# Moving weight loads and low parts in the prologue of a fused attention and FFN kernel, with unread products in two waits

## The reference

```python
# 1 conditional mixing of the 32 tokens, one matrix and bias a sequence
h = gelu(gelu(cond @ W0 + b0) @ W1 + b1)
att = softmax(h @ W2 + b2)                        # 128 x 8
agg_w = einsum('bk,koi->boi', att, weight)        # 128 x 32 x 32
y = einsum('boi,bih->boh', agg_w, x) + (att @ bias_k)[:, :, None]
# 2 causal attention with rope: 32 query heads, 8 key heads of width 16
x = x + attention(y, Wq, Wk, Wv) @ Wo
# 3 grouped convolution over the features, 9 taps, plus cond @ c_weight.T and a bias
z = conv(x) + ctx
# 4 base product, router, low-rank experts
x = x + z @ base_W.T + base_b + lora(z, A, B, router(z))
```

## Time and profile before

| | before |
|---|---|
| median of 3 runs | 616.13 us (613.89 to 617.95) |
| the profiled execution: time | 615.38 us |
| its span, first to last instruction | 613.6 us |
| PE busy | 585.4 us (95%) |
| DVE busy | 494.0 us (81%) |
| ACT, POOL busy | 221.4 us (36%), 226.7 us (37%) |
| DMA, mean | 116 GB/s |

### The profile page before, as it was taken

The page is one execution under the profiler, slowest core; times in us unless marked ns, Lnnn a source line. Parts: engine busy times, 40 slices in busy tenths (PEclk is TensorE's granted clock), DMA queues, the critical chain, the costliest instruction groups (busy, mean ns, idle before and its releaser), DMA issues.

```text
span 613.6 us, 14243 instructions
## 1 busy us (share of the span) xinstructions
PE 585.4 (95%) x4928; PEld 492.8 (80%) x4928; DVE 494.0 (81%) x1236; ACT 221.4 (36%) x603; POOL 226.7 (37%) x182
## 2 busy tenths in 40 slices
PE   4988999999999999999999999999999999999875
PEld 4666798888888988888889888888898878888664
DVE  4677888888888888888888888888888878888843
ACT  4263334333333333333333333333333333333311
POOL 8164234433333344333333443333334333343310
PEclk9989999999999999999999999999999999999999
DMA  7844454344545543445555434454554344554430
GB/s 195 174 115 114 112 134 127 100 101 106 118 116 133 133 121 98 104 106 118 116 133 133 121 99 104 105 118 116 133 133 121 88 107 104 111 133 111 112 86 36
DMA packets 125206, 71.26 MB, mean 116 GB/s; under 512 B 48781, under 2 KB 107309, under 8 KB 125064
## 3 DMA queue, kind: packets, MB, share of 16 engines
q1 hardware_dynamic: 123696, 70.53, 48.0%
q10 hardware_dynamic: 1352, 0.27, 0.3%
q0 software_dynamic: 144, 0.28, 0.2%
HBM read 51.53 MB, written 19.53 MB: 116 GB/s over the span
## 4 chain that ended last, share of the span: by engine, by line
PE 83%; DVE 6%; DMA 5%; issue 2%; ACT 1%; SPq 1%; ACTq 1%; DVEq 0%
PE ps L420 19%; PE ps L576 15%; PE ps L597 10%; PE ps L603 6%; PE ps L623 5%; DMA scratch<-x_dram 5%; PE ps L524 4%; PE ps L615 4%; PE ps L642 4%; PE ps L662 3%; PE ps L561 3%; PE ps L587 2%; PE ps L631 2%; PE ps L564 2%; PE ps L611 1%
## 5 line engine op out<-in xcount | busy, mean ns | idle before, releaser
L957 POOL TENSOR_TENSOR qk<-network,t 128x640 f32<-128x640 f32 x31 | 48.3, 1560 | 161.2 <-DVE t L1143 161.2
L420 PE MATMUL ps<-wqkv_hi,y_hi 128*128 128x512 f32 (+1 forms) x256 | 88.2, 345 | 3.6 <-DVE raw L1162 2.2
L420 PE MATMUL ps<-wqkv_hi,y_lo 128*128 128x512 f32 (+1 forms) x256 | 88.3, 345 | 0.0
L420 PE MATMUL ps<-wqkv_lo,y_hi 128*128 128x512 f32 (+1 forms) x256 | 88.1, 344 | 0.0
L969 POOL TENSOR_TENSOR raw<-x1p,basebB 128x512 f32<-128x512 f32 x32 | 49.5, 1548 | 58.2 <-DVE x1p L1222 58.2
L755 ACT ACTIVATE raw<-ps 128x512 f32<-128x512 f32 x64 | 37.8, 595 | 74.3 <-PE ps L642 74.2
L964 POOL TENSOR_TENSOR raw<-raw,zero 128x512 f32<-128x512 f32 x32 | 33.3, 1041 | 72.1 <-DVE raw L1211 72.1
L420 PEld LDWEIGHTS ps<-wqkv_hi,y_hi 128*128 128x128 f32 x256 | 49.3, 192 | 11.8 <-DVE raw L1162 3.6
L941 POOL TENSOR_TENSOR raw<-raw,rz 128x512 f32<-128x512 f32 x32 | 33.7, 1052 | 56.4 <-DVE rz L1172 56.4
L420 PEld LDWEIGHTS ps<-wqkv_lo,y_hi 128*128 128x128 f32 x256 | 49.3, 193 | 6.2
L420 PEld LDWEIGHTS ps<-wqkv_hi,y_lo 128*128 128x128 f32 x256 | 49.1, 192 | 6.0
(11 more groups left out here) (185 smaller groups left out, 1459.9 us busy)
## 6 DMA issues: line engine op xcount, KB each, us to landing
scratch<-x_dram SPq DMA_DIRECT2D x96, 256.0 KB, 5.8
x_dram<-x1p SPq DMA_DIRECT2D x32, 260.0 KB, 2.1
xm<-x SPq DMA_DIRECT2D x32, 256.0 KB, 4.4
xr<-x SPq DMA_DIRECT2D x32, 256.0 KB, 2.7
out<-raw SPq DMA_DIRECT2D x32, 256.0 KB, 2.0
v_dram<-vS SPq DMA_DIRECT2D x32, 64.0 KB
vB<-v_dram SPq DMA_DIRECT2D x128, 16.0 KB, 4.9
mixb<-mixb_dram SPq DMA_DIRECT2D x28, 64.0 KB, 3.8
```

The lines of the kernel that those rows point to most:

```text
L420: last = mm(dst, a, b, start=(n == 0), stop=(n == 3 * len(left) - 1))
L957: nc.gpsimd.tensor_tensor(qk[:, :], t1, t2[:, :], ALU.add).then_inc(qk_sb, 1)
```

## The change

It touches the head and the periods -1 to 2 alone; the loop and the tail are the same instructions as before.

- Five products of 128 rows by 512 columns whose result no one reads are put on TensorE ahead of the wait for the softmax of the condition (`att_sb`), four behind `mixing_weights`, three behind `prepare_conv`. Their operand is `z_hi`, which DVE sets to zero first.
- POOL's memsets of `vB`, `x1p`, `cvR` and the pads stand ahead of its wait for the mixing tables (`cwS`), and not behind its copies of them.
- DVE: y of group 0 stands ahead of the low part of Wq's third quarter (`prepare_q(2)`), and `y_lo` ahead of `keep_bias`.
- ACT: the copy of the mixing matrices (`keep_mixing_weights`) stands ahead of `prepare_kv`; the DMAs that pass them on stand behind it.
- SP: the load of Wo stands behind the wait for `mixw_in2`. The load of base_W moves from there to behind the one of group 2's x. The load of lora B, four DMAs in the head, becomes one in period 1, with a DVE copy (`order_lora`) that brings it into the order of the transposes. The load of the mixing matrices of groups 4 to 31 moves from ahead of period 0 into period 1.
- `prepare_ar` moves behind `scores(0)` on TensorE, behind the exponentials on ACT and behind `normalize(0)` on DVE. On ACT the values of group 0 are copied ahead of qT.
- `prepare_base`: phases 0 and 1 move from period 0 to the place in period 1 that phases 2 and 3 had, and 2 and 3 move behind `values(1)`.

```diff
-            for j in range(PH):
-                sp.dma_start(rawB[:, j, :, :], loraB.rearrange("e (p j) r -> j p e r", j=PH)[j]).then_inc(ld["B"], 16)
             sp.wait_ge(y_ps, 1)
@@
-            for k in range(NKV):
-                sp.dma_start(rawo[HD * k:HD * (k + 1), :, :],
-                             Wo.rearrange("(k g d) n -> k d g n", k=NKV, g=NQ)[k]).then_inc(ld["wo"], 16)
@@
             sp.wait_ge(mixw_in2, 16 * NB)
-            sp.dma_start(rawbase, baseW.rearrange("(p j) l -> p j l", j=PH)).then_inc(ld["base"], 16)
+            for k in range(NKV):
+                sp.dma_start(rawo[HD * k:HD * (k + 1), :, :],
+                             Wo.rearrange("(k g d) n -> k d g n", k=NKV, g=NQ)[k]).then_inc(ld["wo"], 16)
@@
             sp.dma_start(xm[:, :], group(x_g, 2)).then_inc(xm_in, 16)
+            sp.dma_start(rawbase, baseW.rearrange("(p j) l -> p j l", j=PH)).then_inc(ld["base"], 16)
@@
-            sp.wait_ge(mixw_out, 16)
-            load_mixw(sp, 4, G, mixw_in)
@@
+                if peeled(t, 1):
+                    sp.dma_start(rawB.rearrange("p e j r -> p e (j r)"), loraB.rearrange("e (p j) r -> p e (j r)", j=PH)
+                                 ).then_inc(ld["B"], 16)
+                    sp.wait_ge(mixw_out, 16)
+                    load_mixw(sp, 4, G, mixw_in)
@@ tensor, head
+            pe.wait_ge(zeros_sb, 1)
+            for _ in range(5):
+                mm(ps[:, 5, :], z_hi[:, 0, :], z_hi[:, :, :].rearrange("p j n -> p (j n)"), start=True, stop=True)
             pe.wait_ge(att_sb, 1)
@@ tensor, steps
-                if peeled(t, 0):
-                    prepare_ar()
@@
                     first_bias()
                     mixing_weights()
+                    unread(4)
@@
                 if live(t):
                     scores(t)
-
+                if peeled(t, 0):
+                    prepare_ar()
                 if peeled(t, 1):
-                    prepare_base((2, 3))
+                    prepare_base((0, 1))
@@
                     prepare_conv()
+                    unread(3)
@@
                 if live(t):
                     values(t)
+                if peeled(t, 1):
+                    prepare_base((2, 3))
@@ gpsimd
             nc.gpsimd.memset(mixw[:, :, :, :], 0.0).then_inc(mixw_zero, 1)
+            nc.gpsimd.memset(zero[:, :], 0.0)
+            nc.gpsimd.memset(vB[:, :, :, :], 0.0)
+            nc.gpsimd.memset(x1p[:, :, :], 0.0)
+            nc.gpsimd.memset(cvR[:, :, :, :, :], 0.0).then_inc(cvZ_sb, 1)
@@ vector, steps
                     prepare_q(0)
-                    prepare_q(2)
                     first_mixing_bias()
@@
                 if peeled(t, -1):
+                    prepare_q(2)
+                    first_y_lo()
                     keep_bias()
-                    first_y_lo()
@@
                     softmax(t)
                     normalize(t)
+                if peeled(t, 0):
+                    prepare_ar()
@@
+            def order_lora():
+
+                dve.wait_ge(ld["B"], 16)
+                v.tensor_copy(phB, rawB.rearrange("p e j r -> p j e r")).then_inc(phB_sb, 1)
```

More of the change, by code:

```diff
@@ L291, in base_bank @@
         def base_bank(j):
-            return (6, 5, 6, 7)[j]
+            return (6, 7, 2, 6)[j]
         def z_transposed():
@@ L455, in first_bias, with unread @@
                 mm(ps[:, 4, 0:S], attT[0:NCOND, :], cbiasS[:, :], start=True, stop=True).then_inc(aggb_ps, 1)
+            def unread(products):
+                for _ in range(products):
+                    mm(ps[:, 5, :], z_hi[:, 0, :], z_hi[:, :, :].rearrange("p j n -> p (j n)"), start=True, stop=True)
             def mixing_weights():
@@ L473, in prepare_base @@
                 for j in phases:
-                    if j >= 2:
-                        pe.wait_ge(base_lo_sb, j - 1)
+                    if j == 3:
+                        pe.wait_ge(base_lo_sb, 1)
                     for jo in range(PH):
@@ L651, in values @@
                     pe.wait_ge(hwT_lo_sb, t - 1)
+                if peeled(t, 0):
+                    pe.wait_ge(prep_sb, 1)
                 if peeled(t, 1):
-                    pe.wait_ge(base_lo_sb, PH)
+                    pe.wait_ge(base_lo_sb, 2)
                 pe.wait_ge(pT_sb, 2 * t + 2)
@@ L841, in steps @@
             def steps(t):
+                if peeled(t, 0):
+                    act.wait_ge(rope_t, 2)
+                    keep_values()
                 if live(t):
@@ L847, in steps @@
                     copy(z_hi[:, :, :].rearrange("p j (q o) -> p j q o", o=CG), z_transposed()).then_inc(z_hi_sb, 1)
-                if peeled(t, 0):
-                    act.wait_ge(rope_t, 2)
-                    keep_values()
-                    prepare_ar()
                 if live(t + 1):
@@ L856, in steps @@
                 if peeled(t, -1):
+                    keep_mixing_weights()
                     prepare_kv()
-                    keep_mixing_weights()
+                    pass_mixing_weights()
                 if peeled(t, 2):
@@ L887, in steps @@
                     copy(heads(oT_hi, 0), heads_ps(0)).then_inc(oT_hi_sb, 1)
-                if peeled(t, 0):
-                    prepare_base((0, 1))
+                if peeled(t, 1):
+                    prepare_base((2, 3))
                 if live(t + 1) and not peeled(t, -1):
@@ L1274, in steps @@
                     conv_bias(t)
+                if peeled(t, 1):
+                    prepare_base((2, 3))
+                    order_lora()
                 if live(t - 2) and not peeled(t, G):
```

32 lines of the change are left out of this document (13 added, 19 removed).

## The result

The changed kernel takes 619.96 us, median of 13 runs (617.80 to 623.80), beside 616.77 (612.59 to 619.05) for the kernel before on the same chip: a ratio of 1.007 with a 95% interval of 1.0046 to 1.0093. It is slower by 0.7%, about 4 us (the medians lie 3.2 us apart). The forecast was 613.6 us with a range to 617.4: the wrong side of no change, and outside the range. One execution of the kernel before, timed beside the experiments, took 1261 us and is left out.

A forecast was written before the change was run, and what follows sets the result against it. It took TensorE's queue of products to bound the kernel, with changes only in the first 60 us. A 0.35 loss less 2.9 gain gave -2.55 on 613.6: span 611.05, time 612.8, median 613.6 us after 0.75; range 611.0 to 617.4.

The forecast's parts named there:

- Head: First stretch: attP 0.75 us sooner, y_lo ended at about 16.4, q and k of group 0 ready at 24.2, not 25.96.
- Mixing blocks: Period 0: their store goes at about 17.35 and they are back 6.3 us later, mixw_in2 at 23.7.
- Wo's landing: Period 0: issues from 23.7 to 27.0, landing 3.5 us after the last, at 30.5; ACT waits 3 us.
- the unlikely case: Wo so late that it costs: blocks take 8.9 us, landing 5.6, Wo there at 35.1, time 618 us; chance 0.09.
- From Wo to the softmax: Period 0: wo_hi, POOL's wo_lo and the normalisation sum to 5.75 us; softmax ready at 36.25, not 37.62.
- The clock: Period 0: TensorE idle from 33.2 to 36.3 us, yet the granted clock full from 36 to 42; no loss booked.
- The rival: Clock falls in the new hole of period 0: costs up to 3.6 us, time 614.8 to 617.2; chance 0.23.
- Said start of the product: Period 0: group 0's product with Wo starts at 39.45 instead of 42.37, a gain of 2.9 us.
- Period 1: Eight base-weight transposes, 0.97 us, in a 0.6 us hole between values(1) and the product with Wo: loss 0.35 us.

The follow-up runs named there:

- the repeat: The changed kernel, unchanged, run once more on the same chip as others for a second profile: 619.69 us, ratio 1.0066.
- the tail filled: Ten unread products in the last group's period, ahead of transpose_p(31) and values(31): changed kernel 619.11 us (1.0061), kernel before 614.21 us (0.9983).
- Wo by heads: The changed kernel with Wo loaded at the same place in four DMAs of 128 rows, not eight of 16 partitions: 617.48 us, ratio 1.003.
- the hole filled: The changed kernel with 13 unread products between the keys and values product and the transposes of the probabilities in period 0: 617.07 us, ratio 1.0029.
- the kernel before with Wo late: The kernel before with Wo's load moved behind the wait for mixw_in2, ahead of the load of base_W: 616.88 us, ratio 1.0031.

## Why the prediction was wrong, step by step

**Head: right.** `attP` took 0.22 us (said: 0.2), the blocks' store went at 17.41 (17.35), `y_lo` ended at 16.6 (16.4). Queries(0) then started only at 18.12, behind four unread products at the lower clock (16.61 in the repeat, where the clock had risen by then), and q and k of group 0 were ready at 25.2, 1 us later than said.

**Mixing blocks: right, and better.** Wo's first issue came at 22.92, 0.8 us ahead of the 23.7 of the text.

**Wo's landing: mis-sized.** I took 3.5 us beside little else and wrote 30.5; the source line of the load (duration of the issue, stretch, what waits, landing; before: the earlier trace rows) reads:

```profile
L341 SPq DMA_DIRECT2D raw<-L_attn_Wo x8: 348/426/428, 22.9 to 26.1; - x8
...
  ACT wo_hi L766: 3.3, 1
...
DMA to landing us min/median/max: 2.9/4.6/5.8
```

The landing that counts is that of the last issue, at 26.12: 5.82 us in place of 3.5, so ACT starts at 31.96. The earlier trace rows has 5.6 for a maximum, and I gave it to the unlikely case; other profiles of the changed kernel's order have 6.3 to 6.5. The row above at 28 to 29 us shows why the quiet queue didn't help: eight DMAs of this shape share 150 GB/s at a DMA share of 1.1, so by this rate 1 MB takes some 7 us (an estimate); from the first issue to the last landing it was 9.0. The issues are out after 3.6 us, so it is the transfer that sets the landing. The last issue went 0.9 us earlier than said; what is left is a cost of 1.46 us.

**From Wo to the softmax: right.** Said 5.75 us, measured 37.77 less 31.96, 5.8. The hole was said to be 3.1 us, from 33.2 to 36.3; it was 3.1, from 34.9 to 38.02, since queries(1) started at 30.46 and not at 29.0.

**The clock: the step that failed.** The forecast had TensorE come out of a hole of 3.1 us at full clock and booked nothing for a fall. The rival was named, with its place and the rows that it would show, and given 0.23, against which stood "dense products run right up to this hole". They did, and the clock fell: in both profiles of the changed kernel, without the unread products, with the tail filled and with Wo by heads: five of five profiles with a hole of 3.1 to 5.1 us there, and in none of the four without it. In two of these four the hole, of 2.7 and 2.8 us, stood ahead of the mixing of group 1, and the clock fell behind that one. Over all profiles each wait of TensorE of 2.0 us or more between 24 and 60 us was followed by half clock: twelve of twelve, in eleven profiles, the shortest ones 2.05, 2.14, 2.17, 2.18 and 2.19 us. Waits of 1.1 to 1.8 us were followed by either: the clock stood behind 1.8 us (the hole filled) and 1.6 and 1.2 us (the kernel before with Wo late), and fell behind 1.2 us (`prepare_ar` moved alone). Its price was said to be up to 3.6 us. The product with Wo took 5.46 (said 5.1), the values 1.18 (said 1.3), `transpose_p` 1.95 (said 1.9). At its whole price the rival gave 617.2 us; the 1.46 us of Wo, which it left out, come on top of it.

**The sum put right.** Said start of the product 39.45; Wo 1.46; the end of the softmax 0.25 later to TensorE; the slow clock in transposes, ACT's wait on them and values 1.5: 42.67, the measured one. Then 2.4 us more in the product itself. Against the earlier trace rows the product ends 2.7 us later, and there the forecast had it 2.9 us earlier.

**Period 1: 0.6 and not 0.35.** The transposes took 1.17, not 0.97, and the hole held 0.55 of it. With it the product of group 1 is 3.45 us late, that of group 2 3.2.

**The last 1 to 2 us.** The span grew by 4.4 us and the head explains 3.2. The chain shows the rest in these two profiles: the product with Wo of the last group but one and of the last, before and then now.

```profile
569.62 2.81 PE ps L576 x12
585.89 2.82 PE ps L576 x12
```

```profile
572.59 2.81 PE ps L587 x12
589.87 3.33 PE ps L587 x12
```

The first is 3.0 us late, the second ends 4.5 us late: 1.5 us are the tail, where the clock fell. Such a microsecond, 0.2%, is less than the intervals of the ratios can tell, and the filled tail of the changed kernel (1.0061 beside 1.007) doesn't show it. It is also a question of which execution one compares with: the kernel before ran with mean granted clocks of mostly 0.992 to 1.00, and beside the experiments its runs at 1.00 took 612.9 to 614.0 us, those at 0.992 615.0 to 619.6. The changed kernel had 0.981 to 0.992 in all 13 runs. A mean of 0.989 over 618 us is 13.6 us at half clock (618 x 0.011 / 0.5), and the stretches of its profile add up to that: 10.2 around 38 to 48 us and 3.4 in the tail. Of the kernel before, 0.997 over 614 is 3.7 us, which is about the fall at 34 to 37 us.

**A rule weighed.** The earlier trace rows spoke against the Trainium skill's remark that transposes do not count as busy for the clock (TensorE: Matmul & The Clock Gate, Part 4). The kernel before with the tail filled would fit it: from 26 to 28 us TensorE was busy for 2.00 of 2.00 us, with transposes above all, and the clock was at 0.51 right behind. But the same transposes stand there in all five profiles with this order: in two of them the clock fell right behind (this one, and the kernel before with Wo late, 0.60 at 28 to 30), in three it did not (the kernel before, memsets early, base weights behind the values). So neither, one stretch, nor this one decides the rule. The changed kernel puts such transposes (`prepare_ar`) ahead of queries(1), which ran at full clock; no run tells their part in the fall at 38 us from that of the hole.

## What to carry to other kernels

A load that is moved behind another one's wait is to be priced by the rate that the trace shows for its shape, and by its last landing, and then followed through the queue of the engine that waits for it: here ACT's wait of 3.3 us for Wo stood ahead of the exponentials and became 3.1 us of an idle TensorE. Where an edit makes TensorE idle just ahead of a stretch that is on the path, take the fall of the clock as the likely case and not as the rival; fill the hole or leave the load where it was, and try the parts of the change that need neither (`prepare_ar` and the memsets: 0.3% faster in one comparison, not told from nothing in the next). Compare the mean granted clock of all runs before a microsecond is explained from one profile.

## What the runs showed of the hardware

- The clock can fall under a TensorE that does not stand: 1.00 at 26 to 28 us and 0.51 at 28 to 30, both busy 2.00 of 2.00, in the kernel before with the tail filled. Behind a wait of 2.8 us it stayed at 0.50 from 30 to 34 us although TensorE was busy 4.00 of 4.00. After the hole of 3.1 us it stayed at 0.50 for 10 us, although TensorE was busy 8.4 of them.
- The same instructions lost their clock at different places from profile to profile: one head put group 2's product at 75.92 or 77.42 us, another put group 0's at 39.77 or 40.85. The second pair was taken on two chips; but on each single chip the runs of the kernel before spread from about 613 to over 618 us, too.
- Loads of the same megabyte in two shapes ran at different rates. Wo in eight DMAs of 16 partitions: 150 GB/s at a share of 1.1. In four DMAs of 128 rows of 2 KB: 195 GB/s at a share of 0.51, so half of the engines' time was idle; from the first issue to the last landing 8.3 us in place of 9.0 to 9.8.
- The last of the mixing blocks landed in 1.66 us with nothing beside it; behind Wo's transfers the slowest took 5.6, 6.4 and 6.8 us.
- `attP`, 128 x 16 on DVE, took 0.97 us beside POOL's memsets and 0.22 and 0.23 without them. The first of these memsets, in the kernel before:

```profile
10.62 0.33 POOL L912 MEMSET vB<- 128x256 f32 x1
10.87 0.56 POOL L913 MEMSET x1p<- 128x520 f32 x1
```

  The Trainium skill has a rule of this kind (SBUF — State Buffer, Who interferes with whom): DVE in its two-port mode and GpSimd share a pair of ports, and the one that comes second is blocked for the whole instruction of the other. The trace agrees in that `attP`, issued at 10.86 during the first of them, ended at 11.83, beside the end of the last at 11.87; it was held through several memsets in a row and not through one. No row shows in which mode DVE ran.
